# The loop over the four middle head groups, written out as straight code on every engine

## The reference

```python
Q, K, V = proj(Wq), proj(Wk), proj(Wv)            # each (2, 16 heads, 2048, 16)
# causal softmax over blocks of 128 keys, running maximum and sum
scores = scale * einsum('bhtd,bhsd->bhts', Q, kb)
p = exp(scores - m_new)
acc = corr * acc + einsum('bhts,bhsd->bhtd', p, vb)
O = acc / maximum(l, 1e-12)
x = layernorm(x + O @ Wo.T)
q = round(x / lhs_scale).astype(int8)             # lhs_scale from each row's largest value
x = layernorm(x + (q @ q_rhs) * lhs_scale * rhs_scale)
```

## Time and profile before

| | us |
|---|---|
| median of 3 runs | 1116.11 |
| the three runs | 1112.25, 1116.22, 1116.11 |
| the profiled execution, its own time | 1110.95 |
| its span, first to last instruction | 1109.1 |

### The profile page before, as it was taken

The page is one execution under the profiler, slowest core; times in us unless marked ns, Lnnn a source line. Parts: engine busy times, 40 slices in busy tenths (PEclk is TensorE's granted clock), DMA queues, the critical chain, the costliest instruction groups (busy, mean ns, idle before and its releaser), DMA issues.

```text
span 1109.1 us, 20004 instructions
## 1 busy us (share of the span) xinstructions
PE 1006.8 (91%) x6280; PEld 391.3 (35%) x6280; DVE 822.5 (74%) x1083; ACT 691.9 (62%) x1471; POOL 263.3 (24%) x435
## 2 busy tenths in 40 slices
PE   8999899999999999899899999999998899999972
PEld 5565433333333333233333333333333232344321
DVE  4577776777676767668767776777788898589797
ACT  3444576767666767567666766776665465777730
POOL 4444401020102010120112011201111100555543
PEclk9999999999999999999999999999999899999995
DMA  5666400012011201120102010201021240235501
GB/s 162 208 184 212 121 12 2 7 35 68 5 33 35 65 5 36 31 68 8 35 11 80 14 35 4 81 20 35 6 69 35 73 81 1 46 97 145 154 29 48
DMA packets 71786, 66.39 MB, mean 60 GB/s; under 512 B 15112, under 2 KB 65608, under 8 KB 71684
## 3 DMA queue, kind: packets, MB, share of 16 engines
q1 hardware_dynamic: 71684, 65.10, 21.0%
HBM read 43.25 MB, written 21.35 MB: 58 GB/s over the span
## 4 chain that ended last, share of the span: by engine, by line
PE 72%; DVE 19%; issue 3%; ACT 3%; DMA 1%; POOL 1%; SPq 1%; POOLq 0%; DVEq 0%; ACTq 0%
PE ps_acc L694 22%; PE ps_max L668 20%; PE ps_score L713 18%; DVE block_max L941 11%; PE ps_score L587 5%; PE ps_score L594 2%; ACT PR L893 2%; PE ps_max L671 2%; DVE stats L1055 1%; DMA end_slots<-heads_out 1%; PE ps_acc L568 1%; DVE end_slots L1065 1%; DVE amax L1074 1%; PE ps_max L768 1%; DVE V L1065 0%
## 5 line engine op out<-in xcount | busy, mean ns | idle before, releaser
L941 DVE TENSOR_REDUCE block_max<-ps_max 128x2 f32<-128x1024 f32 (+3 forms) x640 | 655.9, 1062 | 234.8 <-PE ps_max L668 160.2
L893 ACT ACTIVATE PR<-ps_score 128x512 f32<-128x512 f32 (+3 forms) x1280 | 602.7, 536 | 273.0 <-PE ps_score L713 267.7
L713 PE MATMUL ps_score<-QS,KS 99*128 99x512 bf16 (+3 forms) x1280 | 378.5, 352 | 26.6 <-ACT PR L893 18.8
L668 PE MATMUL ps_max<-KS,QS 96*128 96x512 bf16 (+3 forms) x1280 | 358.3, 350 | 41.2 <-DVE block_max L941 38.2
L694 PE MATMUL ps_acc<-PR,VG 128*32 128x512 f32 (+3 forms) x2560 | 301.6, 543 | 0.0
L713 PEld LDWEIGHTS ps_score<-QS,KS 99*128 99x128 bf16 x1280 | 108.2, 97 | 339.7 <-ACT PR L893 236.9
L668 PEld LDWEIGHTS ps_max<-KS,QS 96*128 96x128 bf16 x1280 | 120.7, 98 | 161.0 <-DVE block_max L941 82.0
L1163 POOL TENSOR_SCALAR_AFFINE_SELECT PR<-PR 128x512 f32<-128x512 f32 x128 | 81.3, 636 | 331.5 <-ACT PR L893 331.5
L671 PE MATMUL ps_max<-mask_q,ident_b 128*128 128x128 bf16 x512 | 102.8, 221 | 0.0
L694 PEld LDWEIGHTS ps_acc<-PR,VG 128*32 128x32 f32 x2560 | 50.6, 108 | 95.9 <-ACT PR L893 52.9
L1171 POOL CAST max_parts<-neg_max 16x128 bf16<-16x128 f32 (+1 forms) x31 | 8.8, 283 | 273.0 <-ACT neg_max L876 272.1
(11 more groups left out here) (122 smaller groups left out, 475.3 us busy)
## 6 DMA issues: line engine op xcount, KB each, us to landing
QS<-qparts SPq DMA_DIRECT2D x192, 64.0 KB, 2.3
KS<-kparts SPq DMA_DIRECT2D x192, 64.0 KB, 2.3
qparts<-end_slots SPq DMA_DIRECT2D x16, 384.0 KB, 5.2
kparts<-end_slots SPq DMA_DIRECT2D x16, 384.0 KB, 5.7
PR<-in_L_attn_x SPq DMA_DIRECT2D x8, 512.0 KB, 4.4
heads_out<-accS SPq DMA_DIRECT2D x124, 32.0 KB
end_slots<-in_L_attn_x SPq DMA_DIRECT2D x4, 512.0 KB, 9.7
out_y<-end_slots SPq DMA_DIRECT2D x8, 256.0 KB, 2.1
```

The lines of the kernel that those rows point to most:

```text
L668: m = pe.matmul(bank[:, 0:w], QS[0:STACK, p, i // TPC, j, i % TPC * P:i % TPC * P + P], KS[0:STACK, p, b, j, 0:w], start=True, stop=not diag)
L713: pe.matmul(bank[:, 0:CH - s], KS[:, p, kb // TPC, j, kb % TPC * P:kb % TPC * P + P], QS[0:KROWS, p, c, j, s:CH], start=True, stop=True).t ...
L893: act.activation(PR[:, k % 4, j, 0:w], ps_score[:, score_slot(pos), 0:w], ACT.Exp, scale=SCALE).then_inc(s_exp, 1)
L941: dve.tensor_reduce(block_max[:, h * PAIR:h * PAIR + PAIR, i, b], ps_max[:, slot_at:slot_at + PAIR, 0:w], AX.X, ALU.max).then_inc(s_reduce ...
```

## The change

On each of the five engines the `Fori` loop becomes a Python loop, which writes its body out twice when the program is built. With h a number, g is one too, and each wait and each address in groups 1 to 4 becomes a constant. `wait_apart` then adds no marks, the register operations go, and so do the branch in front of the loop and the one at its end. Tables, tiles, buffers and the order of matmuls, exponentials, reductions and DMAs stay as they are.

```diff
--- before.py
+++ after.py
@@ -516,7 +516,7 @@
                     sp.dma_start(sums_of(row_inv, m), sums[0:sum_rows(m), m % SLOTS, :]).then_inc(e_back[m % SLOTS], 16)
 
                 group(0, 0)
-                with sp.Fori(0, GROUPS // 2 - 2) as h:
+                for h in range(GROUPS // 2 - 2):
                     group(h, 1)
                     group(h + 1, 0)
                 group(GROUPS // 2 - 2, 1)
@@ -804,7 +804,7 @@
                 pe.wait_ge(rest1, QK_UNITS * XCHUNKS)
                 pe.wait_ge(v_copied, 2 * XCHUNKS)
                 group(0, 0)
-                with pe.Fori(0, GROUPS // 2 - 2) as h:
+                for h in range(GROUPS // 2 - 2):
                     group(h, 1)
                     group(h + 1, 0)
                 group(GROUPS // 2 - 2, 1)
@@ -917,7 +917,7 @@
                 front()
                 act.wait_ge(part3, QK_UNITS * XCHUNKS)
                 group(0, 0)
-                with act.Fori(0, GROUPS // 2 - 2) as h:
+                for h in range(GROUPS // 2 - 2):
                     group(h, 1)
                     group(h + 1, 0)
                 group(GROUPS // 2 - 2, 1)
@@ -1044,7 +1044,7 @@
                                 invert_sums(m)
 
                 group(0, 0)
-                with dve.Fori(0, GROUPS // 2 - 2) as h:
+                for h in range(GROUPS // 2 - 2):
                     group(h, 1)
                     group(h + 1, 0)
                 group(GROUPS // 2 - 2, 1)
@@ -1246,7 +1246,7 @@
                         pool.wait_ge(v_copied, 2 * n)
                         values_in(0, n - 1)
                 group(0, 0)
-                with pool.Fori(0, GROUPS // 2 - 2) as h:
+                for h in range(GROUPS // 2 - 2):
                     group(h, 1)
                     group(h + 1, 0)
                 group(GROUPS // 2 - 2, 1)
```

## The result

| | before | after |
|---|---|---|
| median of 5 runs, us | 1115.76 | 1105.25 |
| lowest to highest, us | 1110.75 to 1116.22 | 1103.71 to 1106.33 |
| profiled execution, its own time, us | 1110.95 | 1105.97 |
| its span, us | 1109.1 | 1104.2 |

The ratio is 0.9918, with a 95% interval of 0.9893 to 0.9944. That is 9.1 us of 1115.76, between 6.2 and 11.9. The two medians of five lie 10.51 us apart. The forecast was 1107.6, a factor of 0.9924.

A forecast was written before the change was run, and what follows sets the result against it. The prediction took TensorE to bound the kernel (72% of the chain of waits). Edge 4.67 + registers 3.76 = 8.43 us, a factor of 0.9924 on 1116.11, gave 1107.6 us, with a range of 1100 to 1113.5.

The forecast's parts named there:

- Group 5 as the price of a straight group: Group 5, already straight, does the work of groups 1 to 4; its 111.98 us prices each, 447.92 us for four.
- The edge: Between the loop's two passes, groups 2 and 3: TensorE's taken branch and slow clock after it cost 3.31 + 1.36 = 4.67 us.
- ScalarE's share: ScalarE's branch between the passes costs nothing extra, as its next work waits for TensorE; counted inside the 4.67 us.
- The register part: Groups 1 to 4: waits on registers, at ScalarE's first exponential of a step, cost 0.94 us a group, 3.76 in all.
- in straight code both waits are met without it: At a step's first exponential on ScalarE, straight code needs no register operation for its two waits; 0.08 us less per step.
- Code blocks in straight code: Loading about 24 code blocks on TensorE's queue in groups 1 to 4 was taken to cost nothing beyond group 5's length.
- longer issues: SyncE's DMA issues for KS take 1.2 us more per group in straight code, as much for QS; said to be hidden.
- The slower rival: Late code blocks on TensorE's queue in groups 1 to 4, 4.67 us each; three give +5.6 us, 1121.7 us; chance 0.06.
- The clock falls once more elsewhere: Rival: TensorE's slow clock comes up elsewhere, 3.4 us at most, leaving a net gain of 5.0, 1111.1 us; chance 0.07.

The follow-up runs named there:

- pe_act: Kernel before with the loop made straight code on TensorE and ScalarE only, loops kept on VectorE, GpSimd and SyncE: 1105.87 us, ratio 0.9938.
- drop_straight: Changed kernel without ScalarE's wait on the steps done ahead of a step's first exponential: 1106.07 us, ratio 0.9940 to the kernel before.
- small_loop: Changed kernel plus a three-pass TensorE loop over a met wait and an increment, ahead of group 3: 1105.52 us, ratio 0.9929 to the kernel before.
- open_first: Changed kernel with TensorE's waits for a free score bank moved ahead of others, one mark increment left out: 1105.86 us, ratio 0.9937 to the kernel before.

## Why the prediction was right

- *Group 5 as the price of a straight group* was the step that carried it. The four groups took 447.88 us, predicted 447.92.
- *The edge* was named rightly and sized from one execution, 4.67 us. Over three executions it is 4.67 to 5.7. The bound (3.31 to 4.67) took the case of no slow clock into account, but not the case of more of it, nor of a longer branch. This is the term that was mis-sized, by up to 1.1 us, and with it the forecast of -8.4 stands at the lower end of 8.5 to 9.5.
- *That ScalarE's share is inside the 4.67* was right, and the single-engine runs show it: TensorE's loop alone away leaves 1.33 us of ScalarE's edge; both away leave nothing.
- *The register part*, 3.76 us, came out at 3.8 (4 x (112.92 - 111.97)), but the words for it were half right. The cause is the open wait on an instruction ahead of the exponential, as said. That registers are needed for it is wrong: with the waits changed over, straight code pays 0.83 us per group and loop code 0.16. So is "in straight code both waits are met without it": there too a separate instruction has one of the waits, the one that is met early. That unrolling removes the cost hangs on the order of two lines in the source, which the prediction did not look at.
- *Code blocks in straight code* cost nothing visible (23 on TensorE's queue between 236 and 693 us, about 24 expected), *SyncE's* longer issues neither. The slower rival has nothing in the trace for it.
- *The clock falls once more elsewhere* was a rival with 0.07, but it isn't an alternative. Every profile has such stretches, in places that differ, and in the profiled pair they account for most of the difference between 8.47 and 4.9 us (group 0 and group 6 together 2.89). It is noise on all the cases, and should have been in the range of each rather than a case of its own.
- *The time* fits in part by luck. The forecast is 2.35 us above the median measured, and the gain of 9.1 is the largest of five: the four other kernels whose groups 1 to 4 are straight on TensorE and ScalarE (`pe_act`, `drop_straight`, `small_loop`, `open_first`) gained 6.7 to 7.9 us against 17 to 29 runs of the kernel before, though all but one have the same 447.8 to 447.9 us in these groups (`small_loop` 449.0). The runs' mean granted clock is 0.981 before, and 0.981, 0.980, 0.980, 0.984 and 0.983 for the changed kernel and these four. So in three of the five, slow clock in other places seems to have taken the place of the edge's. Whether straight code brings that on was not tested.

## What to carry to other kernels

If some passes of a loop's work stand as straight code in the same kernel, their length in the profile prices the unrolling before it is done; cut both at the same instruction. A loop with few passes and a long body pays at the taken branch on each engine whose code has to be loaded again, and the stops of several engines lie on top of each other, so that all on the critical path have to go. Where an instruction of an engine that holds up others waits for two semaphores, look at which wait stands on the instruction itself: on ScalarE here it should be the one that is met last. On TensorE the same edit gave nothing.

## What the runs showed of the hardware

- A taken branch costs by the code that it goes back over, as far as these runs show: 3.3 to 4.1 us over two groups on TensorE, with one 16 KB block moving within it each time, 0.21 to 0.24 us over a few instructions, 0.08 us when not taken. On VectorE and GpSimd, with 348 and 232 records in the body, the next record came 0.36 and 0.29 us after a taken branch.
- A wait that is met last costs ScalarE 0.06 to 0.08 us more on an instruction ahead than on the exponential itself (idle time of 0.89 and 0.91 us against 0.83 at a group's start).
- TensorE's clock falls to half for 3.4 or 6.8 us behind idle time in one execution and not behind the same idle time of 1.69 us in the next. 3.4 us of it cost 1.0 us in group 0. It moved single executions of an unchanged kernel by some us, and two profiles of kernels that differ by 8.5 us in the groups by 4.9 us in all.
